# Expert rows of batches 2 and 3: added on VectorE inside the first pass of maxima instead of on GpSimd in front of it

## The reference, cut to what matters

```python
# layer 0, experts (12 experts, top 3): out[token] = sum of its experts' rows
pooled = out.mean(axis=1)                                   # per batch
phi = sigmoid(relu(pooled @ Wp1 + bp1) @ Wp2 + bp2)
out = out * (1.0 - (phi > 0.7) * 0.8)                       # one factor per batch
x = x + out
# layer 1, attention: 16 heads of 16, 4096 keys shared by all batches
Q = (layernorm(x) @ Wq.T)                                   # per batch
scores = Q K^T / 4;  attn = softmax(scores)
```

## Time and profile before

| | us |
|---|---|
| median of 3 runs (lowest, highest) | 2130.94 (2130.51, 2131.64) |
| the profiled execution's own time | 2126.49 |
| its span (first to last instruction) | 2124.7 |
| busy over the span: PE, DVE, ACT, POOL | 1971.0, 1559.4, 1343.0, 287.5 |
| the block around the change: from its first vector addition to the end of the last reduction | 503.4 to 639.3 |
| of it the first pass of maxima (64 reductions) | 543.5 to 639.3 |

### The profile page before, as it was taken

The page is one execution under the profiler, slowest core; times in us unless marked ns, Lnnn a source line. Parts: engine busy times, 40 slices in busy tenths (PEclk is TensorE's granted clock), DMA queues, the critical chain, the costliest instruction groups (busy, mean ns, idle before and its releaser), DMA issues. The chain is left out here.

```text
span 2124.7 us, 40040 instructions
## 1 busy us (share of the span) xinstructions
PE 1971.0 (93%) x15912; PEld 997.2 (47%) x15912; DVE 1559.4 (73%) x1960; ACT 1343.0 (63%) x2648; POOL 287.5 (14%) x292
## 2 busy tenths in 40 slices
PE   6993999995779999999999999999999999998995
PEld 3653889994423333333333333333333333446673
DVE  2537112224889999999999999999999999513454
ACT  1220444441016888888888888888888888783321
POOL 0001334433230000000000000000000000002473
PEclk9995999997568999999999999999999999999997
DMA  4202768764454101103201004101003000001135
GB/s 147 94 21 69 230 219 262 257 214 149 82 85 67 24 6 17 17 7 59 35 6 20 15 7 69 25 7 19 15 7 90 2 7 7 14 24 38 43 102 169
DMA packets 162031, 145.96 MB, mean 69 GB/s; under 512 B 85322, under 2 KB 132406, under 8 KB 161078
## 3 DMA queue, kind: packets, MB, share of 16 engines
q1 hardware_dynamic: 152438, 117.69, 22.4%
q0 software_dynamic: 9408, 25.70, 3.8%
HBM read 108.63 MB, written 32.10 MB: 66 GB/s over the span
## 5 line engine op out<-in xcount | busy, mean ns | idle before, releaser
L1095 DVE TENSOR_REDUCE maxp<-banks 128x2 f32<-128x1024 f32 x1024 | 1235.4, 1224 | 20.9 <-PE banks L1089 19.9
L1698 ACT ACTIVATE pring<-banks 128x512 f32<-128x512 f32 x2048 | 1107.0, 602 | 169.5 <-PE banks L1585 48.4
L1599 PE MATMUL banks<-pring,vcur 128*17 128x256 f32 x8192 | 636.5, 386 | 4.9 <-ACT osb L1692 4.0
L1585 PE MATMUL banks<-qst,kst 50*128 50x512 f32 x2048 | 511.2, 496 | 0.0
L1089 PE MATMUL banks<-kst,qst 50*128 50x512 f32 x2048 | 431.9, 419 | 28.2 <-DVE maxp L1095 21.6
L1585 PEld LDWEIGHTS banks<-qst,kst 50*128 50x128 f32 x2048 | 193.9, 184 | 424.4 <-ACT pring L1698 411.9
L1599 PEld LDWEIGHTS banks<-pring,vcur 128*17 128x17 f32 x8192 | 139.9, 95 | 368.7 <-issue 184.6
L1089 PEld LDWEIGHTS banks<-kst,qst 50*128 50x128 f32 x2048 | 200.3, 192 | 66.4 <-DVE maxp L1095 51.8
L822 ACT ACTIVATE hT<-banks,b 128x128 f32<-128x128 f32 x295 | 107.8, 367 | 188.8 <-PE banks L758 174.0
L960 DVE TENSOR_SCALAR yo<-banks,wblock 128x256 f32<-128x256 f32 x59 | 28.5, 484 | 225.0 <-PE banks L767 225.0
L1567 POOL TENSOR_TENSOR osb<-osb,bc 128x512 f32<-128x512 f32 x15 | 19.2, 1280 | 1151.8 <-DMA bc<-reciprocals 1151.8
(11 more groups left out here) (314 smaller groups left out, 1249.4 us busy)
## 6 DMA issues: line engine op xcount, KB each, us to landing
w1r<-in_L_ffn_w SPq DMA_DIRECT2D x59, 640.0 KB
kst<-key_parts SPq DMA_DIRECT2D x18, 512.0 KB
key_parts<-ksp SPq DMA_DIRECT2D x32, 256.0 KB, 3.0
w2all<-in_L_ffn_w SPq DMA_DIRECT2D x12, 640.0 KB, 7.9
qst<-query_parts SPq DMA_DIRECT2D x96, 64.0 KB
kf<-in_kT SPq DMA_DIRECT2D x16, 256.0 KB
query_parts<-qsp SPq DMA_DIRECT2D x8, 512.0 KB, 2.7
vcur<-in_v SPq DMA_DIRECT2D x16, 256.0 KB, 4.8
```

Of the source, the lines that this page charges most:

```text
L1095: return nc.vector.tensor_reduce(maxp[:, :, hp, qt, kb], ps[:, base:base + 2, :], X, ALU.max)
L1585: nc.tensor.matmul(ps[:, score_bank(n), :], kst[g % 2][rows, j // 2, kt * P:(kt + 1) * P], qst[i][rows, j // 2, :], start=True, stop=True) ...
L1599: mm = nc.tensor.matmul(ps[32 * j:32 * j + VC, 7, cols], vcur[g % 2][:, kt, j, :], pring[:, (G % 2) * HG + j, cols], start=(kt == 0 and ha ...
L1698: nc.scalar.activation(pring[:, n % (2 * HG), :], ps[:, score_bank(n), :], ACT.Exp, scale=float(DH) ** -0.5).then_inc(exp_done, 1)
```

## The change

- POOL no longer adds slabs; `rows_added` and `pool_add` go. DVE adds those of batch 2 in front of the reduction of unit 1 and those of batch 3 in front of that of unit 3 (`ADD`), with the same `add_rows` as for batches 0 and 1.
- The token steps of batches 2 and 3 come two behind one unit, behind units 2, 3, 5 and 6 (before: one each behind units 2 to 5 and 8 to 11).
- The factor of batches 2 and 3 (they share the steps) runs in front of reductions 7 to 16 instead of 12 to 25, the two residuals in front of 17 and 18 instead of 26 and 28.
- The turns of batches 1, 2, 3 come at units 4 to 7, 25 to 28, 43 to 46 (before 6 to 9, 32 to 35, 47 to 50). Their pieces stand three units apart: 13, 16, 19, 22; 31, 34, 37, 40; 49, 52, 55, 58 (before at successive units 23 to 26, 38 to 41, 53 to 56).

```diff
-                POOLED, POOLED_BANK = {2: 2, 3: 8}, 2
-                FAC_AT = 12
-                FACTOR = {FAC_AT + d: i for i, d in enumerate((0, 4, 5, 9, 10, 11, 12, 13))}
-                LATE = {FAC_AT + 14: 2, FAC_AT + 16: 3}
-                PIECE = {u0 + i if i < TB else u1 + i - TB: (b, i) for b, u0, u1 in ((1, 6, 23), (2, 32, 38), (3, 47, 53))
+                ADD = {1: 2, 3: 3}
+                POOLED, POOLED_BANK = {2: (2, 0), 3: (2, 2), 5: (3, 0), 6: (3, 2)}, 2
+                FAC_HIDDEN, FAC_SUMMED = 8, 10
+                FACTOR = {7: 0, 9: 1, 10: 2, 12: 3, 13: 4, 14: 5, 15: 6, 16: 7}
+                LATE = {17: 2, 18: 3}
+                PIECE = {u0 + i if i < TB else u1 + 3 * (i - TB): (b, i) for b, u0, u1 in ((1, 4, 13), (2, 25, 31), (3, 43, 49))
...
-                        for n, c in enumerate((2, 3)):
-                            tiles = slice(TB * c, TB * (c + 1))
-                            pool.wait_ge(erows_in[c], 16 * TOP0)
-                            for k in range(TOP0):
-                                if k:
-                                    pool.wait_ge(pool_add, (TOP0 - 1) * n + k)
-                                w = nc.gpsimd.tensor_tensor(acc[:, tiles, :], acc[:, tiles, :], expert_sums[c][:, k], ALU.add)
-                                w.then_inc(pool_add if k < TOP0 - 1 else rows_added, 1)
...
-                            if c < 2:
-                                pe.wait_ge(erows_done, TB * c + i + 1)
-                            else:
-                                pe.wait_ge(rows_added, c - 1)
+                            pe.wait_ge(erows_done, TB * c + i + 1)
...
                         for u in range(NU):
+                            if u in ADD:
+                                add_rows(ADD[u])
                             if u in FACTOR:
```

More of the change, by code:

```diff
@@ L1130, in build @@
                 erows_in = l1_sems(" ".join(f"erows_in{c}" for c in range(NB)))
-                erows_done, rows_added, pool_add, pooled_mm, pooled_done, gp_done, phi_done, phi_mm, ephi_done, fac_done = l1_sems(
-                    "erows_done rows_added pool_add pooled_mm pooled_done gp_done phi_done phi_mm ephi_done fac_done")
+                erows_done, pooled_mm, pooled_done, gp_done, phi_done, phi_mm, ephi_done, fac_done = l1_sems(
+                    "erows_done pooled_mm pooled_done gp_done phi_done phi_mm ephi_done fac_done")
                 keys_in1, = l1_sems("keys_in1")
                 FEW = KEYS // 4
-                POOLED, POOLED_BANK = {2: 2, 3: 8}, 2
-                FAC_AT = 12
-                FACTOR = {FAC_AT + d: i for i, d in enumerate((0, 4, 5, 9, 10, 11, 12, 13))}
-                LATE = {FAC_AT + 14: 2, FAC_AT + 16: 3}
-                PIECE = {u0 + i if i < TB else u1 + i - TB: (b, i) for b, u0, u1 in ((1, 6, 23), (2, 32, 38), (3, 47, 53))
+                ADD = {1: 2, 3: 3}
[4 more added lines that the diff above has]
+                PIECE = {u0 + i if i < TB else u1 + 3 * (i - TB): (b, i) for b, u0, u1 in ((1, 4, 13), (2, 25, 31), (3, 43, 49))
                          for i in range(TB + KD * KD)}
@@ L1304, in _ @@
                             max_unit(first_unit(u), 0, kst[0], 4 + 2 * (u % 2)).then_inc(max_mm, 1)
[L1305 to L1312, removed]
+                            if u in POOLED:
+                                c, i0 = POOLED[u]
+                                if (c, i0) == (2, 0):
+                                    pe.wait_ge(q_left, KD)
+                                for i in range(i0, i0 + 2):
+                                    mm = pool_tokens(c, i, POOLED_BANK)
+                                if (c, i0) == (NB - 1, 2):
+                                    mm.then_inc(pooled_mm, 1)
+                            if u == FAC_HIDDEN:
                                 hidden_factor(2, 2, NB, POOLED_BANK)
-                            if u == FAC_AT + 7:
+                            if u == FAC_SUMMED:
                                 summed_factor(2, 2, NB, POOLED_BANK)
```

## The result

| | median, us | runs | profiled execution, us | its span, us |
|---|---|---|---|---|
| before, first shown | 2130.94 | 3 | 2126.49 | 2124.7 |
| before, in the comparison | 2131.64 (2128.74 to 2135.77) | 7 | | |
| changed | 2139.14 (2137.51 to 2139.41) | 7 | 2139.14 | 2137.4 |

The ratio is 1.0033, 95% interval [1.0023, 1.0043]: slower by 7.5 us. The two profiled executions lie 12.65 apart, because the profiled one of before (2126.49) was shorter than any of its seven runs.

A forecast was written before the change was run, and what follows sets the result against it. DVE was taken to bound the pass, though not full, waiting only for PE's scores. The pass grows by 19.3 us, less 6.4 in front: +12.9, so the median of 2130.9 becomes 2143.8 us, range 2133 to 2149.

The forecast's parts named there:

- in front of the pass: Ahead of the pass of maxima: without POOL's six additions batch 1's slabs go faster, 6.4 us won, bounds 4.3 and 8.6.
- additions on DVE: In the pass: two batches of additions at 3.95 us stand between DVE's reductions while PE waits, +7.9 us.
- beside POOL's `xn`: Batch 2's additions on DVE take turns with batch 1's four `xn` on POOL: +4.7 us, bounds 0 and 4.85.
- token steps, factor, batch 1's pieces: First reduction to batch 2's residual: waits in the new order sum to 8.0 us against 8.3, about -0.3.
- pieces of batches 2 and 3: Pieces three units apart, most at 1.2 GHz: 8.0 us of waits against 5.2, +2.8, bounds -5.2 and +5.7.
- two stalls for `xn`: At units 25 and 43 PE reaches the turn before POOL's `xn`, waiting 2.1 us each: +4.2, bounds 0 and 4.9 for both.
- A quarter at 2.4: Lone pieces of batches 2 and 3: a quarter expected at 2.4 GHz, most at 1.2, giving 8.0 us of waits.
- From profile to median: Whole kernel: the median lies 4.4 us above the profiled execution, so 2139.4 becomes 2143.8.
- clock up: Lone pieces keep PE's array at 2.4 GHz, -8.0 us, turns and token steps -1: net +4, 2135; chance 0.18.
- a wash: `xn` doesn't block additions, half the pieces run at 2.4 GHz, stalls half vanish: +3.4, 2130 to 2134 us; chance 0.12.
- Faster: DVE's waits in the pass swallow the additions; pass stays near 96 us, 6.4 in front kept: 2124.5; chance 0.06.
- No gain in front: The query load sets the pass's start, so only about 0 to 3 of 6.4 us come: 2147 to 2150; chance 0.06.

The follow-up runs named there:

- the additions alone: Changed kernel with token steps, factor, residuals, turns and pieces back at the units of before, additions staying on DVE in the pass: 2132.35 us, ratio 1.0013 to before.
- the second profile of before: The kernel before, word for word, profiled once more in a single execution: 2133.4 us.
- the placement alone: Changed kernel with the additions of batches 2 and 3 back on POOL in front of the pass, new places kept: 2142.36 us, ratio 1.0050 to before.

## Why the prediction was right, and where not

The direction held, and all mechanisms but one. Against the profiled execution it forecast 2139.4, and the changed kernel has 2139.14; but its median was forecast at 2143.8. Step by step, all against the profiles:

| term | forecast | measured |
|---|---|---|
| in front of the pass | -6.4 | -6.4 (543.49 to 537.13; the block began 0.7 later, so 7.0 within it) |
| additions on DVE | +7.9 | +7.7 (2 x 3.85) |
| beside POOL's `xn` | +4.7 | +0.5 (4.34 - 3.85) |
| token steps, factor, batch 1's pieces | -0.3 | -0.2 (what the other rows leave of the pass's 18.3) |
| pieces of batches 2 and 3 | +2.8 | +5.7 (8 x 1.36 = 10.9, for 5.2) |
| two stalls for `xn` | +4.2 | +4.2 (2 x 2.09) |
| batch 2's residual, beside a product of POOL | 0 | +0.4 (1.69 for 1.27) |
| sum | +12.9 | +11.9; the profiled executions differ by 12.65, about 0.8 of it behind the pass |

**In front and additions:** right; the additions alone give the same 537.0. That the front came out at exactly 6.4 is partly luck, as the second profile of before, with its front of 38.1, shows.

**Beside POOL's `xn`: the step that failed.** It held that "DVE waits as well", for the `xn` in progress, and took 4.7 from `vareps` at 0.43 instead of 0.17. The row itself may well have been read rightly: `vareps` ends with the `xn`, 591.50 and 591.48, and another small one-input step of DVE also ends with an operation of POOL, in the first profile of before:
```profile
580.07 1.27 POOL L1172 TENSOR_TENSOR qsp<-qf,qsp 128x512 fp32r<-128x512 f32 x1 [30.52 <-ACT qf L1167]
580.42 0.93 DVE L1377 TENSOR_SCALAR fac<-fac 128x2 f32<-128x2 f32 x1
```
(`fac` takes 0.16 alone; in the second profile it takes 0.64 and again ends with POOL's product.) The failure was to carry this from a small one-input step over to two-input additions. Beside an `xn` those lose 0.24 on two large and 0.24 on four small ones; POOL loses 1.6. The row with POOL's `xn` at 2.12 pointed the right way. Why the two kinds of DVE operation differ no run here shows. The Trainium skill has one more rule on this ("SBUF — State Buffer", "🔬 SBUF: two separate sides"): the shared pair is an exclusive lock, held for the whole instruction, and the other blocks. For POOL the trace agrees (its `xn` waited), and DVE's small steps would fit; for DVE's additions it does not, as 0.24 is no whole `xn` of 1.21. The measurement decides.

**Pieces:** the mechanism was right, the size not. "A quarter at 2.4" was a hedge; none were, so the strict reading beside it (all eight at 1.2 GHz) was the better one. The two errors, -4.2 and +2.9, nearly cancel, and the good sum owes something to that.

**From profile to median: also wrong.** The prediction added the 4.4 us between the profiled before and its median to both kernels. They are no constant: the kernel before varies (2123.04 to 2135.77 over the comparisons of this study, one run of 2444.47 aside), while the changed kernel keeps within 1.9 us and its own profile is its median. Part of that is what the rows of pieces cost when the clock rises late: the second profile's span is 6.9 longer than the first's (2131.6 and 2124.7), with 4.3 more in the pass, 2.0 less in front, 1.5 more ahead of the block and 3.0 more behind the pass. That a clock that never rises makes a kernel steady is not shown: the placement alone, whose clock stays at 0.50 in the pass too, spreads over 8.5 us. Against the second profile of before the changed kernel's pass ends 8.0 later (651.2 and 643.2) and its execution takes 5.7 more (2139.14 and 2133.4); the medians lie 7.5 apart.

**The rivals:** *clock up* did not come. Of *a wash* one part did, the additions beside `xn`. *Faster* fell, though its idea is half true: at the old places the additions cost 2 us by the medians, since what they cost in the pass is won back in front. *No gain in front* fell at 537.13.

What stays open: which work ahead of a row of pieces lets the clock rise in it, and what moves the part behind the pass, which is the same code in all these kernels and took 1485.3 to 1492.5 in their profiles.

## What to carry to other kernels

Where work moves onto the engine that a pass waits for, price it against what it frees elsewhere: here 8.2 in the pass against 5.0 to 7.0 in front, about 2 us by the medians, while a second edit in the same change, the new places, left the pieces without the clock, put two turns ahead of their `xn`, and cost the rest. The helper engine was not wrong for the additions, only its hour was: put behind the work that it collided with, it kept them and won 5 to 6 us. And when a price hangs on where in a stretch the clock rises, profile the kernel before twice; one profile may be its lucky one.

## What the runs showed of the hardware

- Beside one-input work on GpSimd, six two-input additions on VectorE lost 0.5 us in all, and GpSimd waited instead (4.85 to 6.47 for four); with two-input work on GpSimd six additions took 5.28 instead of 3.85.
- Small one-input operations on VectorE (128x2 and 128x4) lasted until the end of the GpSimd operation beside them: `fac` 0.93 and 0.64 instead of 0.16, `vareps` 0.43 instead of 0.17.
- Reductions from PSUM were not slowed by GpSimd's two-input additions (8.64 for seven, each 1.23 as elsewhere).
- One program had its clock rise in batch 2's second piece in one execution and in its last in another; the two passes differ by 4.3 us.
- A four-piece row at 1.2 GHz costs 5.86, spaced 5.44; with a rise in it 2.5 to 2.8 when the rise comes early, 3.9 to 5.1 when it comes late.
- A race decides 2 us: VectorE's two large additions took 2.48 when its second had begun before GpSimd's first (by 0.03), and 4.55 when GpSimd's began first (by 0.12).
